# Router scores with the centroids as the stationary side and 512 tokens moving, turned back by TensorE

## The chip, the cores and the metric

One core of one Trainium2 chip runs the whole program in one launch. The metric is the device time of that core in microseconds, the median of several executions; lower is better.

## The reference, cut to what matters

The model takes 1024 tokens of 256 features and passes them through a feed-forward layer, attention, a second feed-forward layer, a mixture of experts, a Mamba layer and the same mixture of experts again. Ahead of each stands a layer norm. The change touches the router of the two mixtures:

```python
shared = _swiglu(x, wg_s, wu_s, wd_s) * RATIO
affinity = jax.nn.sigmoid(jnp.einsum('bsh,eh->bse', x, centroids))
biased = affinity + gate_bias
_, top_idx = jax.lax.top_k(biased, K)
top_aff = jnp.take_along_axis(affinity, top_idx, axis=-1)
weights = top_aff / (top_aff.sum(-1, keepdims=True) + EPS)
...
for e in range(E):
    routed = routed + mask[..., e:e + 1] * _swiglu(x, wg[e], wu[e], wd[e])
```

Here x is the normalised input, E is 16 experts, K is 2, and there are 256 features.

## The kernel before, in words

All engines walk one list of steps, `plan`, in the same order; each engine's program picks the steps it has a part in. So the order of the list is the order of every engine's queue. A step is a tuple such as `("route", u, ch)`: u is 0 for the first mixture and 1 for the last, ch is the half of the tokens (512 each, in TC = 4 tiles of 128).

A layer norm of one half is the steps of `norm_steps`: `stat` (VectorE, line 1561 and 1563: mean and variance of four tiles), `rstd` (GpSimd), `nrm` (VectorE, line 1574: four tiles, in two steps of two), `tr` (TensorE, line 489: eight 128x128 turns into two PSUM banks) and two `xn` (ScalarE, line 1326, copies a bank to `XN` as the high part; VectorE, line 1581, makes the low part from the difference). Products are made from high and low parts: `three` gives the pairs high-high, low-high, high-low, so a product over 256 features takes six matmuls (`group`, line 485).

`moe_steps(u)` orders the router. `mld` loads the centroids (VectorE splits them into `Cn`, 16 columns per 128 features) and the shared experts' weights. `route` is TensorE's: for each of four tiles six matmuls with the tokens' 128x128 tile of `XN` as the stationary side and the 16 centroid columns moving, 24 matmuls in all, so that the scores come out as 128 tokens by 16 experts in `bank(ch)`. `top` is ScalarE's sigmoid of 128x64 into `aff` (line 1375), and then VectorE's add of the bias (line 1687), the eight largest (line 1690) and their indices (line 1694). `rank` makes the one-hot rows (VectorE) and counts with 44 small matmuls (TensorE); `pos` turns the counts into row numbers (VectorE, lines 1716 to 1735). `scat` then writes the tokens to their experts' rows in memory, `GX`, by 16 indirect transfers that GpSimd issues one after another (lines 2005 and 2011). `fetch` (SyncE) reads them back, and `e1` to `e4` run the experts. Beside the scatter, the shared experts run: `sgu`, `smid`, `sdn`, and `sadd` (VectorE, line 1780) adds them to X. The first turn of `e1` waits for the first fetch and for `sadd`.

Before the change, the list is: `route` of half 0, the whole norm of half 1, `top` of half 0, then `route`, `top` and the rest of half 1.

Of the kernel before, what the change touches and what calls it, by code (L numbers as in the profile page):

```python
# [6 lines left out]
F = mybir.dt.float32  # L7
# [259 lines left out]
def moe_steps(u):  # L267
    s = 3 + 2 * u
    yield [("mld", u)]
    later = norm_steps(s, 1)  # L270
    yield [("route", u, 0)]
    for x in later:
        yield x
    yield [("top", u, 0)]
    yield [("route", u, 1), ("top", u, 1), ("rank", u), ("wsp", u)]
    yield [("sgu", u, 0, 0), ("pos", u), ("scat", u), ("wts", u)]
    yield [("sgu", u, 0, 1), ("smid", u, 0, 0), ("sgu", u, 1, 0), ("smid", u, 0, 1), ("sdn", u, 0, 0)]
    yield [("sgu", u, 1, 1), ("smid", u, 1, 0), ("sdn", u, 0, 1), ("smid", u, 1, 1), ("sdn", u, 1, 0), ("sdn", u, 1, 1)]
    yield [("sadd", u), ("fetch", u, 0), ("fetch", u, 1)]
    aside = iter([[x] for k in range(len(MW)) for x in (("mwl", k), ("mws", k))]) if u == 0 else iter(())  # L280
    n = len(PAIRS)
    for i in range(n + 3):
        if i < n:
            yield [("e1", u, i)]
            b = PAIRS[i][1]
            gi = (b - 1) // WB
            if i % 2 == 0:
                yield [("ids", u, gi)]
            if (b % WB == 0 or b == NB) and gi + 2 < len(GROUPS):
                yield [("fetch", u, gi + 2)]  # L290
        if 0 <= i - 1 < n:
            yield [("e2", u, i - 1)]
        if 0 <= i - 2 < n:
            yield [("e3", u, i - 2)]
        if 0 <= i - 3 < n:
            yield [("e4", u, i - 3), ("back", u, i - 3)]
        yield next(aside, [])
    after = norm_steps(4, 0)
    for h in range(NT // 2):
        yield [("yload", u, h)]  # L300
    for t in range(NT):
        yield [("comb", u, t)]
        if u == 0 and t >= TC:
            yield next(after)
    if u == 0:
        yield from after
        yield from norm_steps(4, 1)
# [111 lines left out]
def build(nc, d):  # L419
# [11 lines left out]
    with ctx:  # L431
# [3 lines left out]
        def sig(name, keys, step=1):  # L435
            return Sig(ctx.enter_context(nc.semaphore(name)), keys, step)
# [58 lines left out]
        ldc, ldb = sig("s_ld_cst", [()], 16), sig("s_ld_b16", [()], 16)  # L495
        pset = sig("s_pool_set", [("ones",), ("minus",), ("none",), ("mhalf",), ("zero",), ("b2h",)])
        gz = sig("s_gx_rows", [(0, "zero"), (0, "spare"), (1, "copy")], 16)
        asum = sig("s_abs", of("abs"))
        qsum = sig("s_abs_sum", of("sum"))
        wq = sig("s_wquant", of("quant"))  # L500
        con = sig("s_const", [()])
        var = sig("s_var", of("rstd"))
# [13 lines left out]
        tld = sig("s_ld_rope", [()], 16)  # L516
        awh, awq = sig("s_wqkvo_hi", [()]), sig("s_wqkvo", [()])
        vset = sig("s_v_pads", [()])
        kset = sig("s_k_pads", [()], 64)
# [45 lines left out]
        cen = sig("s_cen", of("mld"))  # L565
        rtd = sig("s_route", of("route"))
        sgm = sig("s_sigmoid", of("top"))
        hotd = sig("s_onehot", of("rank"))
# [125 lines left out]
        cenw = fa.take(32)  # L694
        bufs = [fa.take(CH) for _ in range(4)]
        small = Area(fa.take(1100), 1100)
        xin = [fa.take(WB * RW) for _ in range(2)]
# [63 lines left out]
        def sync_program():  # L761
            for x, *a in plan:
# [10 lines left out]
                elif x == "qld":  # L773
                    sp.wait_ge(*con.at())
                    sp.dma_start(wst, d["qkvo"]).then_inc(*qld.inc())
# [97 lines left out]
        def tensor_program():  # L873
# [31 lines left out]
            for x, *a in plan:  # L905
# [61 lines left out]
                elif x == "pj":  # L967
# [3 lines left out]
                    if (ch, w, u) == (0, "q", 0):  # L971
                        pe.wait_ge(*xad.at(0, 1))
                        pe.wait_ge(*awq.at())
                    for v in range(2):
# [18 lines left out]
                elif x in ("diag", "off"):  # L993
# [3 lines left out]
                    if x == "diag" and i == 0:  # L997
                        pe.wait_ge(*plc["q", g // 2].at(ch))
                        pe.wait_ge(*plc["k", g // 2].at(ch))
                        if ch:  # L1000
                            pe.wait_ge(*mzd[ch, g].at(ch, g))
                        if g == ch == 0:
                            pe.wait_ge(*kset.at())
                            pe.wait_ge(*qzero.at())
                            pe.wait_ge(*con.at())

# [63 lines left out]
                elif x == "route":  # L1070
                    u, ch = a
                    s = 3 + 2 * u
                    if ch == 0:
# [3 lines left out]
                        else:  # L1077
                            pe.wait_ge(*mlx.at(TC - 1))
                    pe.wait_ge(*xno.at(s, ch, 1))
                    for i in range(TC):  # L1080
                        A = [xn(k, ch, i * P, i * P + P) for k in range(2)]
                        t = group(bank(ch)[:, i * 16:i * 16 + 16], [q for k in range(2) for q in three(A[k], [w[:, k, :] for w in Cn])])
                    t.then_inc(*rtd.inc(u, ch))
                elif x == "rank":
# [6 lines left out]
                elif x == "sgu":  # L1091
# [3 lines left out]
                    if k0 == 0:  # L1095
                        pe.wait_ge(*wsl.at(u, 0))
                        pe.wait_ge(*sgm.at(u, 1))
                    elif k0 == 1:
                        pe.wait_ge(*posd.at(u))
                    else:  # L1100
                        pe.wait_ge(*smd.at(u, n - 1, ch))
# [212 lines left out]
        def scalar_program():  # L1314
            for x, *a in plan:
# [51 lines left out]
                elif x == "attT":  # L1367
# [3 lines left out]
                    act.activation(XN[:, 0, :, ch, :], bk, ACT.Copy).then_inc(*ath.inc(ch))  # L1371
                elif x == "top":
                    u, ch = a
                    act.wait_ge(*rtd.at(u, ch))
                    act.activation(aff[:, ch * TC:ch * TC + TC, :], bank(ch)[:, 0:16 * TC].rearrange("p (t e) -> p t e", e=16), ACT.Sigmoid).then_inc(*sgm.inc(u, ch))
                elif x == "wsp":
# [136 lines left out]
        def vector_program():  # L1513
# [6 lines left out]
            for x, *a in plan:  # L1520
# [17 lines left out]
                elif x == "const":  # L1538
# [3 lines left out]
                    dve.tensor_copy(TRI[:, :], b16[:, 256:512])  # L1542
                    dve.tensor_copy(BC16[:, :], b16[:, 0:256]).then_inc(*con.inc())
                elif x == "stat":
# [52 lines left out]
                elif x == "wq":  # L1597
                    dve.wait_ge(*awh.at())
                    dve.tensor_tensor(Wall[1], wst, Wall[0].bitcast(F), ALU.subtract).then_inc(*awq.inc())
                elif x == "rp1":  # L1600
# [18 lines left out]
                elif x == "vadd":  # L1619
# [4 lines left out]
                    if ch == n == 0:  # L1624
                        dve.wait_ge(*vset.at())
                    for v in range(2):
# [57 lines left out]
                elif x == "top":  # L1684
                    u, ch = a
                    dve.wait_ge(*sgm.at(u, ch))
                    dve.tensor_tensor(bi[:, ch * TC:ch * TC + TC, :], aff[:, ch * TC:ch * TC + TC, :], cst("gb").unsqueeze(1).broadcast_to([P, TC, 16]), ALU.add).then_inc(*d_own.inc())
                    dve.wait_ge(*d_own.at())
# [255 lines left out]
        def gpsimd_program():  # L1944
            for x, *a in plan:
# [26 lines left out]
                elif x == "wo":  # L1972
# [3 lines left out]
                    pool.wait_ge(*p_own.at())  # L1976
                    pool.memset(vv[:, :, 17:32], 0.0).then_inc(*vset.inc())
                elif x == "xbo":
# [157 lines left out]
```

## Time and profile before

| what | value |
|---|---|
| median of 3 runs | 938.44 us (932.56 to 939.86) |
| span of the profiled execution | 936.1 us |
| TensorE busy with matmuls | 713.1 us, 76% |
| VectorE, ScalarE, GpSimd busy | 592.4, 371.6 and 347.5 us |
| mean granted TensorE clock | 0.864 |

The span runs from the first to the last instruction of one execution. No time of that same execution from outside is among the numbers; its span lies 2.3 us under the median of the three runs and inside their spread. A granted clock of 1.0 is 2.4 GHz and one of 0.5 is 1.2 GHz.

### The profile page before, as it was taken

What the parts mean: (1) busy time and instruction counts of PE and PEld (TensorE: products, weight loads), DVE (VectorE), ACT (ScalarE), POOL (GpSimd) and SP (SyncE); (2) the same over time, 40 slices, a digit from 0 to 9 for tenths busy, and PEclk for the clock granted to TensorE, in tenths of its full rate; (3) what the DMA queues carried; (4) which work ended last, traced back from release to release, by engine and by line L of the source; (5) the groups of instructions that cost most, each with busy time, mean ns of one, the idle gap of its engine ahead of it and who ended that gap; (6) DMA issues with size and microseconds to landing.
All of it is one profiled execution on the core that took longest, in us unless ns stands there. A gap on an engine that the chain in (4) does not pass through costs nothing. (4 is left out here: it accounts for less than half of the span.)

```text
span 936.1 us, 11120 instructions
## 1 busy us (share of the span) xinstructions
PE 713.1 (76%) x3706; PEld 492.4 (53%) x3706; DVE 592.4 (63%) x1012; ACT 371.6 (40%) x754; POOL 347.5 (37%) x422
## 2 busy tenths in 40 slices
PE   3887887889885987599248578888778879675990
PEld 2766453444333766488146345545445545564880
DVE  6868445767522776344367686788988798662333
ACT  4411334255563322033124844586544444130330
POOL 3223222201112202536310055566656667124462
PEclk9989677779888895899769679999999999867995
DMA  4945622020001910364400000000051000103435
GB/s 179 284 62 94 82 36 37 2 35 2 1 1 55 392 35 13 122 184 165 146 1 0 1 0 1 1 1 1 1 216 54 1 0 1 35 24 129 129 123 174
DMA packets 37640, 65.98 MB, mean 70 GB/s; under 512 B 11618, under 2 KB 27618, under 8 KB 35954
## 3 DMA queue, kind: packets, MB, share of 16 engines
q1 hardware_dynamic: 33074, 52.89, 20.1%
q0 software_dynamic: 4512, 12.39, 3.7%
q8 instruction: 31, 0.51, 0.2%
q14 instruction: 23, 0.19, 0.1%
HBM read 39.65 MB, written 21.69 MB: 66 GB/s over the span
## 5 line engine op out<-in xcount | busy, mean ns | idle before, releaser
L1260 PE MATMUL PS<-FB,C 128*128 128x512 f32 x256 | 134.5, 621 | 4.2 <-DVE FB L1919 3.8
L1360 ACT ACTIVATE FA<-PS 128x512 f32<-128x512 f32 (+3 forms) x192 | 80.7, 496 | 71.5 <-PE PS L1030 71.1
L2045 POOL TENSOR_TENSOR FB<-FB,RBF 128x512 f32<-128x512 f32 x51 | 65.8, 1289 | 81.8 <-DVE FB L1910 81.8
L489 PE MATMUL PS<-C,FB 128*128 128x128 f32 x250 | 45.3, 305 | 57.2 <-DVE FB L1574 30.8
L1996 POOL TENSOR_SCALAR_AFFINE_SELECT FA<-FA 128x128 f32<-128x128 f32 x128 | 36.4, 295 | 129.1 <-ACT FA L1360 126.9
L2026 POOL DMA_INDIRECT GY<-FB x62 | 60.7, 979 | 53.7 <-issue 27.5
L1642 DVE TENSOR_REDUCE FA<-PS 128x2 f32<-128x1024 f32 (+2 forms) x64 | 68.0, 1086 | 19.6 <-PE PS L1009 19.4
L489 PEld LDWEIGHTS PS<-C,FB 128*128 128x128 f32 x250 | 35.6, 158 | 68.5 <-DVE FB L1574 30.9
L1030 PE MATMUL PS<-RA 64*128 64x512 f32 (+3 forms) x192 | 60.2, 496 | 5.4 <-ACT FA L1360 4.9
L1153 PE MATMUL PS<-WE,FB 128*128 x248 | 61.0, 390 | 0.0
L2036 POOL TENSOR_TENSOR FB<-WE,FB 128x512 f32<-128x512 f32 x32 | 42.4, 1325 | 49.3 <-ACT FB L1468 49.3
L1260 PEld LDWEIGHTS PS<-FB,C 128*128 128x128 f32 x256 | 45.9, 198 | 21.1 <-issue 11.8
L1030 PEld LDWEIGHTS PS<-RA 64*128 64x128 f32 x192 | 29.1, 222 | 52.7 <-ACT FA L1360 30.3
L485 PE MATMUL PS<-XN,RB 128*128 128x512 f32 x192 | 52.5, 433 | 2.3 <-issue 2.3
L1790 DVE TENSOR_TENSOR FB<-FB,PS 128x256 f32<-128x256 f32 (+1 forms) x32 | 13.2, 413 | 64.2 <-ACT FB L1398 52.0
L1009 PE MATMUL PS<-RA 64*128 64x128 f32 (+3 forms) x288 | 49.7, 385 | 4.7 <-DVE FA L1642 2.7
L1044 PE MATMUL PS<-FA 128*32 128x512 f32 (+3 forms) x384 | 47.8, 576 | 4.0 <-POOL FA L1996 3.9
L1153 PEld LDWEIGHTS PS<-WE,FB 128*128 128x128 f32 x248 | 46.1, 196 | 6.1 <-issue 0.8
L485 PEld LDWEIGHTS PS<-XN,RB 128*128 128x128 f32 x192 | 40.1, 212 | 12.6 <-issue 3.2
L1249 PEld LDWEIGHTS PS<-RBF,WE 128*128 128x128 f32 x256 | 35.5, 203 | 20.4 <-DVE FB L1910 7.5
L1326 ACT ACTIVATE XN<-PS 128x512 fp32r<-128x512 f32 x24 | 13.5, 594 | 76.5 <-PE PS L489 76.5
L485 PE MATMUL PS<-XN,W1Q 128*128 128x512 f32 x128 | 39.3, 445 | 5.1 <-DVE XN L1581 3.6
(265 smaller groups left out, 1628.1 us busy)
## 6 DMA issues: line engine op xcount, KB each, us to landing
WE<-in_wr SPq DMA_DIRECT2D x8, 1536.0 KB, 11.3
FB<-GX SPq DMA_DIRECT2D x14, 520.0 KB
RA<-RA SPq DMA_DIRECT2D x48, 128.0 KB, 4.8
FB<-GY SPq DMA_DIRECT2D x8, 512.0 KB, 5.7
GX<-GX SPq DMA_DIRECT2D x1, 4030.0 KB, 27.6
GX<-FA SPq DMA_DIRECT2D x1, 3968.0 KB, 16.7
FA<-in_w SPq DMA_DIRECT2D x2, 1024.0 KB, 7.0
FA<-in_qkvo SPq DMA_DIRECT2D x1, 1536.0 KB, 20.6
```

The source lines that it names most:

```text
L485: last = pe.matmul(out, a, b, start=start and i == 0, stop=stop and i == len(pairs) - 1, skip_group_check=skip)
L489: return pe.matmul(out, in_, ident, start=True, stop=True, is_transpose=True)
L1009: return pe.matmul(out, QT[r, 2 * g + hh // 2, ii * P:ii * P + P], KT[r, 2 * g + hh // 2, c0:c1], start=start, stop=stop, skip_group_check ...
L1030: pe.matmul(bk[:, c0:CH], KT[r, 2 * g + hh // 2, kt * P:kt * P + P], QT[r, 2 * g + hh // 2, c0:CH], start=True, stop=True).then_inc(*scs.i ...
L1044: t = pe.matmul(bank(7)[32 * hh:32 * hh + 32, c0:CH], V[:, kt, (4 * g + hh) * 32:(4 * g + hh) * 32 + 32], PT[(first_of + hh) % 12][:, c0:C ...
L1153: m = pe.matmul(bk[:, o:o + D], xt[:, o + k * P:o + k * P + P], WE[:, bass.ds(v + k * 256, 256)], start=k == 0, stop=k == 1)
L1260: pe.matmul(bank(m), ident, shc[k % 4], start=n == 0, stop=n == DN - 1).then_inc(*yad.inc(ch, n, m))
L1360: act.activation(PT[n % 12][:, c0:], bank(ring_bank[(x, *a)])[:, c0:], ACT.Exp, scale=0.25).then_inc(*exd.inc(*a))
L1642: r = dve.reduce_max(N3[c0 // CH][:, i, h:h + 2 * hpb].rearrange("p (h b) -> p b h", b=2), bk[:, :, 0:hpb * n].rearrange("p b (h n) -> p b ...
L2026: pool.indirect_dma_start(GY, bass.IndirectOffsetOnAxis(ap=ids[:, b:b + 1], axis=0), yout[pi % 4][:, (b - b0) * D:(b - b0) * D + D], None) ...
L2036: pool.tensor_tensor(sbb[k % 2], uu[ch][:, m, :], bs[(stb.no[ch, n] - 1) % 2], ALU.mult).then_inc(*bmd.inc(ch, n, m))
L2045: pool.tensor_tensor(shc[k % 4], sh[k % 5], Cs[(stc.no[ch, n] - 1) % 2], ALU.mult).then_inc(*cma.inc(ch, n, m))
```

## The change

The router's product is turned round. `route` now takes the 16 centroid columns as the stationary side and moves 512 tokens past them: six matmuls for each half, with a result of 16 experts by 512 tokens. ScalarE takes the sigmoid of that 16x512 block (into `affT`, a part of two buffers that are free then). In `top`, TensorE turns the block back, four turns of 16x128 to 128x16, and VectorE adds the bias to the turned affinities in PSUM, copies them to `aff` for later use, and makes the choices as before. In the list, the statistics and both `nrm` steps of half 1 now stand right after `route` of half 0, and `top` of half 0 stands ahead of `tr` and both `xn`. Some semaphores are merged into others; each wait still names the same event.

```diff
-    later = norm_steps(s, 1)
     yield [("route", u, 0)]
-    for x in later:
-        yield x
-    yield [("top", u, 0)]
+    stat0, stat1, rstd, nrm0, nrm1, tr, xn0, xn1 = norm_steps(s, 1)
+    yield stat0 + stat1 + rstd + nrm0 + nrm1
+    yield [("top", u, 0)] + tr + xn0 + xn1
     yield [("route", u, 1), ("top", u, 1), ("rank", u), ("wsp", u)]
...
-        rtd = sig("s_route", of("route"))
-        sgm = sig("s_sigmoid", of("top"))
+        rtd = sig("s_route", [x for x in plan if x[0] in ("route", "top")])
+        sgm = sig("s_sigmoid", of("route"))
+        afd = sig("s_affinity", of("top"))
...
+        affT = [b[0:16, :] for b in bufs[2:4]]
...
                     pe.wait_ge(*xno.at(s, ch, 1))
+                    group(bank(ch)[0:16, :], [q for k in range(2) for q in three([w[:, k, :] for w in Cn], xn(k, ch))]).then_inc(*rtd.inc(x, u, ch))
+                elif x == "top":
+                    u, ch = a
+                    pe.wait_ge(*sgm.at(u, ch))
                     for i in range(TC):
-                        A = [xn(k, ch, i * P, i * P + P) for k in range(2)]
-                        t = group(bank(ch)[:, i * 16:i * 16 + 16], [q for k in range(2) for q in three(A[k], [w[:, k, :] for w in Cn])])
-                    t.then_inc(*rtd.inc(u, ch))
+                        t = pe.matmul(bank(ch)[:, i * 16:i * 16 + 16], affT[ch][:, i * P:i * P + P], ident[0:16, 0:16], start=True, stop=True, is_transpose=True)
+                    t.then_inc(*rtd.inc(x, u, ch))
...
                     if k0 == 0:
                         pe.wait_ge(*wsl.at(u, 0))
-                        pe.wait_ge(*sgm.at(u, 1))
+                        pe.wait_ge(*afd.at(u, 1))
...
-                elif x == "top":
+                elif x == "route":
                     u, ch = a
-                    act.wait_ge(*rtd.at(u, ch))
-                    act.activation(aff[:, ch * TC:ch * TC + TC, :], bank(ch)[:, 0:16 * TC].rearrange("p (t e) -> p t e", e=16), ACT.Sigmoid).then_inc(*sgm.inc(u, ch))
+                    act.wait_ge(*rtd.at(x, u, ch))
+                    act.activation(affT[ch], bank(ch)[0:16, :], ACT.Sigmoid).then_inc(*sgm.inc(u, ch))
...
-                    dve.wait_ge(*sgm.at(u, ch))
-                    dve.tensor_tensor(bi[:, ch * TC:ch * TC + TC, :], aff[:, ch * TC:ch * TC + TC, :], cst("gb").unsqueeze(1).broadcast_to([P, TC, 16]), ALU.add).then_inc(*d_own.inc())
+                    turned = bank(ch)[:, 0:16 * TC].rearrange("p (t e) -> p t e", e=16)
+                    dve.wait_ge(*rtd.at(x, u, ch))
+                    dve.tensor_tensor(bi[:, ch * TC:ch * TC + TC, :], turned, cst("gb").unsqueeze(1).broadcast_to([P, TC, 16]), ALU.add).then_inc(*d_own.inc())
+                    dve.tensor_copy(aff[:, ch * TC:ch * TC + TC, :], turned).then_inc(*afd.inc(u, ch))
```

## Rows read from the trace of the kernel before

**Rows 1.** Chain that ended last, last mixture: start us, us, what.

```profile
809.66 3.18 DMA FB<-in_cen
...
813.32 4.54 PE PS L485 x24
...
821.48 5.30 PE PS L485 x24
826.80 0.23 ACT FB L1375
...
834.28 0.72 POOL FB L2002
...
857.92 3.52 DMA FB<-GX
```

**Rows 2.** Timeline, first mixture: start us, us, engine, line, op, tiles, count, idle before.

```profile
348.82 4.27 PE L485 MATMUL PS<-RB,XN 128*128 128x16 f32 x24 [3.61 <-DVE RB L1518]
...
352.39 1.38 DVE L1574 TENSOR_SCALAR FB<-X,FB 128x256 f32<-128x256 f32 x4 [1.48 <-POOL FB L1964]
...
353.18 1.97 PE L489 MATMUL PS<-C,FB 128*128 128x128 f32 x8
...
355.60 1.29 DVE L1581 TENSOR_TENSOR XN<-PS,XN 128x512 fp32r<-128x512 f32 x2 [1.83 <-ACT XN L1326]
...
356.94 5.29 PE L485 MATMUL PS<-RB,XN 128*128 128x16 f32 x24 [1.80 <-DVE XN L1581]
...
357.62 0.23 DVE L1687 TENSOR_TENSOR FB<-FB,C 128x64 f32<-128x64 f32 x1 [0.73 <-ACT FB L1375]
...
358.84 0.17 DVE L1694 FIND_INDEX8 FB<-FB 128x8 uint32<-128x16 f32 x1
...
362.53 0.23 DVE L1687 TENSOR_TENSOR FB<-FB,C 128x64 f32<-128x64 f32 x1 [3.52 <-ACT FB L1375]
```

**Rows 3.** Stretches, TensorE alone: us, busy (count), granted clock, DMA share, GB/s.

```profile
349.80:350.00 0.20, 0.20 (x4) 0.91 0.95 323
...
350.00:370.20 20.20, 15.73 (x101) 0.50 0.03 12
...
370.20:386.00 15.80, 14.72 (x84) 0.99 0.23 84
```

**Rows 4.** Timeline, shared experts' first and third `sgu`, on TensorE and ScalarE.

```profile
363.97 1.28 ACT L1385 ACT_TABLE_LOAD   x1
...
366.01 7.85 PE L485 MATMUL PS<-XN,RB 128*128 128x512 f32 x24
...
368.96 0.60 ACT L1385 ACTIVATE FB<-PS 128x512 f32<-128x512 f32 x1 [3.70 <-PE PS L485]
...
374.94 3.06 PE L485 MATMUL PS<-XN,RB 128*128 128x512 f32 x12 [1.08 <-issue]
...
376.64 0.60 ACT L1385 ACTIVATE FB<-PS 128x512 f32<-128x512 f32 x1 [3.55 <-PE PS L485]
```

**Rows 5.** Groups by line and shape: count, busy us, mean ns, idle before.

```profile
L1352 ACT ACTIVATE RA<-PS 8x512 fp32r<-8x512 f32 x8 | 4.7, 587 | 22.1 <-PE PS L489 22.1
...
L485 PE MATMUL PS<-W1Q,RB 128*64 128x512 f32 x16 | 5.9, 442 | 0.0
```

**Rows 6.** Timeline, four turns and the copy behind them, first and last mixture.

```profile
401.72 0.57 PEld L489 LDWEIGHTS PS<-C,FB 128*128 128x128 f32 x4
...
402.57 0.60 ACT L1392 ACTIVATE FB<-PS 128x512 f32<-128x512 f32 x1
...
861.48 1.57 PEld L489 LDWEIGHTS PS<-C,FB 128*128 128x128 f32 x8 [10.63 <-DMA FB<-GX]
...
862.64 0.60 ACT L1392 ACTIVATE FB<-PS 128x512 f32<-128x512 f32 x1 [16.64 <-PE PS L489]
```

**Rows 7.** Timeline, end of the first mixture's scatter and start of its experts.

```profile
393.91 2.74 DVE L1780 SCALAR_TENSOR_TENSOR X<-PS,X 128x256 f32<-128x256 f32 x8 [9.72 <-remote]
...
397.23 1.97 PE L489 MATMUL PS<-C,FB 128*128 128x128 f32 x8 [10.71 <-DMA FB<-GX]
```

More of the change, by code:

```diff
@@ L495, in build @@
         ldc, ldb = sig("s_ld_cst", [()], 16), sig("s_ld_b16", [()], 16)
-        pset = sig("s_pool_set", [("ones",), ("minus",), ("none",), ("mhalf",), ("zero",), ("b2h",)])
+        pset = sig("s_pool_set", [("ones",), ("minus",), ("none",), ("mhalf",), ("zero",), ("b2h",), ("vpad",)])
         gz = sig("s_gx_rows", [(0, "zero"), (0, "spare"), (1, "copy")], 16)
@@ L499, in build @@
         qsum = sig("s_abs_sum", of("sum"))
-        wq = sig("s_wquant", of("quant"))
-        con = sig("s_const", [()])
+        wq = sig("s_wquant", of("quant") + [("const",), ("qkvo",)])
         var = sig("s_var", of("rstd"))
@@ L516, in build @@
         tld = sig("s_ld_rope", [()], 16)
-        awh, awq = sig("s_wqkvo_hi", [()]), sig("s_wqkvo", [()])
-        vset = sig("s_v_pads", [()])
+        awh = sig("s_wqkvo_hi", [()])
         kset = sig("s_k_pads", [()], 64)
@@ L773, in sync_program @@
                 elif x == "qld":
-                    sp.wait_ge(*con.at())
+                    sp.wait_ge(*wq.at("const"))
                     sp.dma_start(wst, d["qkvo"]).then_inc(*qld.inc())
@@ L972, in tensor_program @@
                         pe.wait_ge(*xad.at(0, 1))
-                        pe.wait_ge(*awq.at())
+                        pe.wait_ge(*wq.at("qkvo"))
                     for v in range(2):
@@ L1004, in tensor_program @@
                             pe.wait_ge(*qzero.at())
-                            pe.wait_ge(*con.at())
+                            pe.wait_ge(*wq.at("const"))
                     def score(out, ii, hh, c0, c1, start, stop):
@@ L1542, in vector_program @@
                     dve.tensor_copy(TRI[:, :], b16[:, 256:512])
-                    dve.tensor_copy(BC16[:, :], b16[:, 0:256]).then_inc(*con.inc())
+                    dve.tensor_copy(BC16[:, :], b16[:, 0:256]).then_inc(*wq.inc("const"))
                 elif x == "stat":
@@ L1598, in vector_program @@
                     dve.wait_ge(*awh.at())
-                    dve.tensor_tensor(Wall[1], wst, Wall[0].bitcast(F), ALU.subtract).then_inc(*awq.inc())
+                    dve.tensor_tensor(Wall[1], wst, Wall[0].bitcast(F), ALU.subtract).then_inc(*wq.inc("qkvo"))
                 elif x == "rp1":
@@ L1624, in vector_program @@
                     if ch == n == 0:
-                        dve.wait_ge(*vset.at())
+                        dve.wait_ge(*pset.at("vpad"))
                     for v in range(2):
@@ L1976, in gpsimd_program @@
                     pool.wait_ge(*p_own.at())
-                    pool.memset(vv[:, :, 17:32], 0.0).then_inc(*vset.inc())
+                    pool.memset(vv[:, :, 17:32], 0.0).then_inc(*pset.inc("vpad"))
                 elif x == "xbo":
```

## The prediction

> **What bounds the kernel now.** I read the chain that ended last first, because one router stands in each mixture and only its share of the chain can be won. In the last mixture the chain goes from the load of the centroids through the first scores, the norm of half 1, the 24 matmuls of the second scores (5.30 us), ScalarE's sigmoid and the choices to GpSimd's first piece of the scatter, and from the scatter to the fetch [rows 1]. The second `route` is thus wholly on the path, and what is saved between the end of `xn` and the bias add moves the scatter, the fetch and all behind them. The first mixture has the same shape, and there I read the timeline piece by piece [rows 2]. VectorE ends the low parts at 355.60 + 1.29 = 356.89, TensorE's 24 matmuls run from 356.94 to 362.23, and the bias add starts at 362.53. From 356.89 to 362.53 are 5.64 us. That is the stretch the change rebuilds, twice in the program; the last mixture's has the same 5.29 us or so of TensorE in it [rows 1].
>
> Next I looked at the clock, since a matmul's price depends on it. It falls from 1.0 at about 350.0, one microsecond into the first `route`, after TensorE had been idle 3.61 us [rows 2, 3]. It then stays at 0.5 (1.2 GHz) until 370.2, 4.2 us after the first `sgu` began, and is 0.99 after that [rows 3, 4]. So the second `route` and all that stands beside it run at 1.2 GHz.
>
> **The second half's scores, on the path.** What goes is 5.64 us. What comes, in order:
>
> - Six matmuls of 512 columns. `sgu` has just such a group of six for its gate: at 1.2 GHz it starts at 366.01 and ScalarE takes its result at 368.96, 2.95 us; at 2.4 GHz it starts at 374.94 and is taken at 376.64, 1.70 us [rows 4]. Their stationary side has 128 columns, the new one 16. The nearest row with fewer columns is the one with 64, at 442 ns mean duration and 5.9 us for 16, which is 0.37 us each and lies between the two speeds of the full-width group (0.49 and 0.28 us per matmul with start and drain in it) [rows 4, 5]. I take no gain and no loss from the width. With 0.05 us from VectorE to TensorE (356.89 to 356.94 [rows 2]) this is 3.00 us.
> - The sigmoid of 16x512. ScalarE's cost follows the columns and not the partitions: 8x512 from PSUM takes 587 ns, 128x512 takes 0.60 [rows 4, 5]. I take 0.60, and 0.05 again for the way to TensorE.
> - Four turns of 16x128. No row has this form. The nearest is the four 128x128 turns of `e1`: from the first weight load to the copy behind them 1.16 us at 1.2 GHz (861.48 to 862.64) and 0.85 us at 2.4 GHz (401.72 to 402.57) [rows 6]. The new ones load as many columns (128) but move 16 in place of 128. From below they can't be quicker than the 24 loads of the old `route`, which had the same 128 columns to load and 16 to move: 5.29/24 = 0.22 us each, 0.88 us for four [rows 2]. The range is 0.9 to 1.2; I take 1.15, since start and drain are not in the 0.88.
> - The add of 128x64 costs what it did (0.23 us), now from PSUM. Behind it comes the copy to `aff`, of the same size, ahead of the maxima in VectorE's queue: at most another 0.23 us, less some overlap; I take 0.20 [rows 2].
>
> The sum is 3.00 + 0.60 + 0.05 + 1.15 + 0.20 = 5.00 us, against 5.64: 0.64 us saved in each mixture at 1.2 GHz, 1.3 us in both. With the lower bound for the turns and a copy half hidden it is 1.0 each; with a new group slower by a quarter of its matmul time (0.7 us) it is a loss of 0.1 each.
>
> The Trainium skill has a rule that speaks against the change (TensorE: Matmul & The Clock Gate, section on LDWEIGHTS): a weight load costs its columns divided by 1.2 in ns, whatever the clock, here 107 ns. By that, 24 loads would be 2.6 us, the six long matmuls would win nothing and the change would lose its sigmoid, turns and copy, over a microsecond. The trace does not agree: the old group took 0.22 us for each load and matmul at 1.2 GHz.
>
> **The first half's scores, beside other work.** TensorE's 24 matmuls there end at 353.09, and the turns of the norm start at 353.18, when VectorE has two of its four tiles [rows 2]; in the last mixture `route` ends at 817.86 and the turns follow at once, so there it may hold them up by 0.1 us [rows 1]. The new group starts at the same 348.8, gets its first microsecond or so at 2.4 GHz and ends after about 2.2 us, at 351.0 (2.95 at the latest, 351.8). The sigmoid is then done by 351.7 (352.4), the turns by 352.8 (353.6). ScalarE is free in this stretch. Its table for the sigmoid costs 1.28 us, but a table load does not wait for the data: the one for Silu stands at 363.97, five microseconds ahead of the result it serves at 368.96 [rows 4]. So it goes into ScalarE's idle time before 348.8. TensorE is then free at 352.8 for the norm's turns, which can't start before 353.1. I cost all this at nothing; if that cover were gone, the late sum (353.6) would hold the norm's turns up by 0.5 us per mixture.
>
> **Where VectorE's choices for half 0 go.** They took from 357.62 to 359.01, 1.39 us, beside the second `route`, where VectorE had nothing else [rows 2]. Now they and the copy, 1.6 us, stand between `nrm` (ends 352.39 + 1.38 = 353.77) and the first low part (355.60), where VectorE idled 1.83 us for ScalarE's high part [rows 2]. From 353.77 they end at 355.37, which leaves 0.2 us. Behind VectorE's new wait for the turned scores are queued both low parts, and TensorE's second `route` waits for those. I cost it at nothing, and each tenth beyond 0.2 us goes straight onto the path.
>
> **What hangs behind.** GpSimd starts the scatter when the positions are there, and is its own bound from then on: 16 issues in a row. SyncE's fetch follows the last, and the experts start at 397.23 when it lands [rows 7]. All that is relative to the choices and moves with them. The shared experts' `sgu` also starts earlier by as much. One stretch is not clear: `sadd` starts at 393.91 after 9.72 us of waiting for something the profile does not name, and ends at 396.65, 0.58 us ahead of the fetch [rows 7]. If that wait hangs on the scatter, it moves too; if it hangs on something that stays, no more than 0.58 us can be won in this mixture, nearly all of my 0.64. Merged semaphores cost nothing: no wait has a new event.
>
> The profiled execution's span is 936.1 us; less 1.3 and a tenth for the last mixture's turns it is 934.7. Its span lies 2.3 under the median of 938.44, so the median becomes 937.0.
>
> **The rivals.** First, the clock comes back during the second `route`. The old group ran 5.29 us without a rise [rows 2, 3]. For it: the clock rose 4.2 us after `sgu` began, with matmuls of just the new length [rows 3, 4]. Against it: the new group lasts only some 2.6 us and then TensorE pauses for ScalarE. At 2.4 GHz the stretch is 0.05 + 1.70 + 0.60 + 0.05 + 0.85 + 0.20 = 3.45 us, 2.2 saved in each mixture, 4.4 in all: 934.0. The Trainium skill's rule (TensorE: Matmul & The Clock Gate, Part 1) that the clock is low by default and that activity releases it would allow this; the rise during `sgu` agrees, the level during the old `route` shows that not every busy stretch does it.
>
> Second, slower: VectorE's queue. If the turned scores of half 0 come later than 354.0, so that choices and copy (1.6 us) end after 355.60, the low parts wait. It decides from a chain of 5.2 us from 348.8 on; my late sum of 353.6 is 0.4 short of it. Should narrow-sided matmuls cost half as much again (6 x 0.64 in place of 0.43 us, 1.3 more for a group), the scores of half 0 would come at 354.9, the low parts 0.9 us late (354.9 + 1.6 against 355.60), and the second half's group would be 1.3 us longer, against 0.64 saved: 1.6 us lost in each mixture, 3.1 in all, 941.5. The row with 64 columns speaks against it [rows 5].
>
> Third, the change does what it says but `sadd` or the experts' start holds the place: nothing moves, 938.4.
>
> **How the numbers follow.** Forecast 0.62; clock back, 934.0, 0.15; VectorE's queue, 941.5, 0.08; nothing moves, 0.15. Around each lies the spread of the runs, 7.3 us for three of them, and the time at which the clock rises in later stages can shift by some microseconds with any edit. All four cases are within 1% (9.4 us), which is about what a measurement of this kernel can tell from no change. Beyond it lie only disturbed medians: 0.04 faster, 0.03 slower. For 8 in 10 the range takes in 934.0 less the spread's lower half and 937.0 and 938.4 plus a little of the upper: 930.5 to 940.5; most of the slower rival is left out.
>
> **What would show it.** In the profile after: two groups of six 128x512 matmuls with 16 stationary columns per mixture, the second at a granted clock of 0.5, with ScalarE's sigmoid some 2.95 us behind its start; sigmoid 0.6 us; the bias add 4.8 us after the end of the low parts; the choices of half 0 ahead of the low parts with idle time before the latter under 0.3 us; the experts' first turns about 0.6 us nearer to the centroids' load. A clock of 1.0 there, or low parts that wait for VectorE's own choices, would make me wrong, and so would a `sadd` that ends after the fetch.

## The result and the profile after

The changed kernel takes 929.11 us in the median (924.94 to 932.21, 8 runs) against 937.64 for the kernel before beside it (931.94 to 939.86, 8 runs). The ratio is 0.9918, with a 95% interval of 0.989 to 0.9947: 5.0 to 10.3 us faster, where 1.4 us was forecast. The profiled execution took 925.12 us and its span is 923.8 us. It happens to be one of the quickest, so the difference of the two spans, 12.3 us, is not the gain.

The first mixture's router in the changed kernel's timeline (start us, us, engine, line, op, tiles, count, idle before; PS stands for PSUM banks, PEld is TensorE loading its stationary side):

```profile
343.02 2.69 PE L484 MATMUL PS<-XN,RB 128*16 128x512 f32 x6 [3.73 <-DVE RB L1520]
...
345.75 0.59 ACT L1377 ACTIVATE FB<-PS 16x512 f32<-16x512 f32 x1 [7.12 <-PE PS L484]
...
346.38 0.60 PE L1084 MATMUL PS<-C,FB 16*128 16x16 f32 x4 [0.68 <-ACT FB L1377]
346.58 1.38 DVE L1576 TENSOR_SCALAR FB<-X,FB 128x256 f32<-128x256 f32 x4 [1.47 <-POOL FB L1968]
...
347.88 0.22 DVE L1690 TENSOR_TENSOR FB<-PS,C 128x64 f32<-128x64 f32 x1
348.01 0.22 DVE L1691 COPY FB<-PS 128x64 f32<-128x64 f32 x1
...
349.80 1.29 DVE L1583 TENSOR_TENSOR XN<-PS,XN 128x512 fp32r<-128x512 f32 x2 [0.54 <-ACT XN L1328]
...
351.14 2.74 PE L484 MATMUL PS<-XN,RB 128*16 128x512 f32 x6 [1.80 <-DVE XN L1583]
...
353.92 0.59 ACT L1377 ACTIVATE FB<-PS 16x512 f32<-16x512 f32 x1 [3.67 <-PE PS L484]
...
354.56 0.61 PE L1084 MATMUL PS<-C,FB 16*128 16x16 f32 x4 [0.68 <-ACT FB L1377]
...
355.20 0.23 DVE L1690 TENSOR_TENSOR FB<-PS,C 128x64 f32<-128x64 f32 x1 [4.12 <-PE PS L1084]
355.34 0.22 DVE L1691 COPY FB<-PS 128x64 f32<-128x64 f32 x1
355.47 0.40 DVE L1694 MAX8 FB<-FB 128x8 f32<-128x16 f32 x4
```

Read it against [rows 2]. From the end of the low parts (349.80 + 1.29 = 351.09) to the bias add at 355.20 VectorE is idle for 4.12 us by its row, where the stretch was 5.64 and I had summed 4.80 to that point. The sum's terms, one by one: the group is taken 2.78 us after its start (351.14 to 353.92; I had 2.95), the sigmoid is 0.59, and from the first turn to VectorE's add are 0.64 us, where I had 1.15. The copy, for which I had 0.20, costs the path 0.01: the maxima start 0.27 us after the add (355.20 to 355.47), and in the kernel before, without a copy, they start 0.26 us after it (362.53 to 362.79), since they wait for the add's result in both:

```profile
362.79 0.41 DVE L1690 MAX8 FB<-FB 128x8 f32<-128x16 f32 x4
```

The choices of half 0 start at 347.88, in VectorE's own order behind the four tiles, and VectorE is idle 0.54 us before the low parts: the queue holds nobody up.

The chain that ended last, at the last mixture's router (start us, us, what), and two lines of the timeline there:

```profile
799.65 1.55 DMA FB<-in_cen
...
809.25 2.75 PE PS L484 x6
812.02 0.60 ACT FB L1377
812.66 0.62 PE PS L1084 x4
813.31 0.23 DVE FB L1690
```

```profile
801.69 1.55 PE L484 MATMUL PS<-XN,RB 128*16 128x512 f32 x6 [2.53 <-DVE RB L1520]
...
806.05 1.30 PE L488 MATMUL PS<-C,FB 128*128 128x128 f32 x8 [1.71 <-DVE FB L1576]
```

Against [rows 1], three things are shorter, not one. The scores go as in the first mixture. But the load of the centroids takes 1.55 us in place of 3.18, though nobody touched it. And the norm's turns take 1.30 us where the first mixture needs 1.97 [rows 2]: they run at 2.4 GHz. The stretches with TensorE alone (us, busy, count, granted clock, DMA share, GB/s), first the kernel before, then the changed one, both from just after the split of the centroids:

```profile
813.60:817.60 4.00, 4.00 (x23) 0.57 0.01 4
```

```profile
802.00:806.00 4.00, 1.66 (x10) 1.00 0.35 136
```

What became of the load is told by the list of transfers in that stretch (queue, kind: packets, MB, share; then issues with KB and us to landing), again before and after:

```profile
q1 hardware_dynamic: 430, 0.80, 47.3%
q8 instruction: 1, 0.02, 1.3%
...
FB<-in_cen SPq DMA_DIRECT2D x1, 16.0 KB, 3.2
```

```profile
q1 hardware_dynamic: 432, 0.80, 46.9%
...
FB<-in_cen SPq DMA_DIRECT2D x1, 16.0 KB, 1.6
```

In the kernel before, one packet of instructions crosses the load; in the changed one there is none. That became the first theory to test: the edit took 28 matmuls with their weight loads out of TensorE's program ahead of this point (the first mixture's two halves have 10 each in place of 24), and so moved the packet away.

### The profile page after: what moved, and what is told of

Read it like the earlier page. It is cut to its first block and busy times, and to the rows that moved or that the text cites. A ratio compares the mean times of both kernels' runs of the same rounds, so it can differ in the third digit from the quotient of the medians.

```text
span 923.8 us, 11012 instructions
## 1 busy us (share of the span) xinstructions
PE 697.1 (75%) x3650; PEld 472.3 (51%) x3650; DVE 594.7 (64%) x1016; ACT 372.4 (40%) x754; POOL 351.2 (38%) x422
## 5 line engine op out<-in xcount | busy, mean ns | idle before, releaser
L484 PE MATMUL PS<-XN,RB 128*128 128x512 f32 (+1 forms) x216 | 61.1, 441 | 12.0 <-DVE RB L1520 8.3
L1029 PE MATMUL PS<-RA 64*128 64x512 f32 (+3 forms) x192 | 57.6, 466 | 5.2 <-ACT FA L1362 5.1
L484 PEld LDWEIGHTS PS<-XN,RB 128*128 128x128 f32 (+1 forms) x216 | 41.8, 198 | 26.8 <-DVE RB L1520 9.6
L1251 PE MATMUL PS<-RBF,WE 128*128 128x128 f32 x256 | 37.3, 293 | 6.0 <-DVE RBF L1914 3.6
```

Source lines behind the costliest of these rows:

```text
L484: last = pe.matmul(out, a, b, start=start and i == 0, stop=stop and i == len(pairs) - 1, skip_group_check=skip)
L1029: pe.matmul(bk[:, c0:CH], KT[r, 2 * g + hh // 2, kt * P:kt * P + P], QT[r, 2 * g + hh // 2, c0:CH], start=True, stop=True).then_inc(*scs.i ...
L1251: t = pe.matmul(bank(4 + k % 2)[:, i * P:i * P + P], DUT[ch][i][:, m * P:m * P + P], dg[:, i * P:i * P + P], start=True, stop=True)
```

## The experiments

Twelve runs in three groups of four, four of them repeats; each group shares its runs of the kernel before (medians 935.95, 936.72 and 933.62 us). My theory: 1.5 us in each mixture by the scores, the last mixture's load and clock, and nothing else. The rivals: the merged semaphores, the order of the steps, or something that acts ahead of the first router, where the two profiles already differ by 5.8 us (first statistics of the first mixture at 348.71 and 342.91).

**Merged semaphores alone.**

```diff
-        wq = sig("s_wquant", of("quant"))
-        con = sig("s_const", [()])
+        wq = sig("s_wquant", of("quant") + [("const",), ("qkvo",)])
...
```

> Only the merged semaphores, with the old router. Theory 1 (the gain is made between the end of the low parts and the scatter, 1.5 and 2.1 us in the two profiles, and what lies beyond is the clock of stages that the change does not touch): no change, ratio 1.000 within 0.003, and the stages before the first router (chain at the first bias of the centroids, 348.36 before and 342.56 after) differ from both kernels only as one execution differs from another. Theory 2 (the merged semaphores shorten the waits of the first feed-forward layer and attention): the kernel is 4 to 6 us faster, ratio 0.994 to 0.996, and reaches the first router near 342.5.

936.79 us, ratio 1.0018 (0.9985 to 1.0051): no gain. Its profile nevertheless reaches the first statistics at 343.53.

**The order alone.**

```diff
     yield [("route", u, 0)]
-    for x in later:
-        yield x
-    yield [("top", u, 0)]
+    yield stat0 + stat1 + rstd + nrm0 + nrm1
+    yield [("top", u, 0)] + tr + xn0 + xn1
```

> Only the order: old router, statistics and both norm steps of half 1 ahead of the choices of half 0, which stand ahead of the turns. The old scores of half 0 end 4.3 to 4.5 us after their start and the sigmoid is 0.2 us, so the choices start when VectorE has finished its four tiles, as in the changed kernel, and end before the low parts. Theory 1: no gain from the order, 0 to -0.2 us in each mixture, ratio 1.000 within 0.003. Rival (the order is what gains, since VectorE is free beside the second scores): 1 to 3 us faster.

937.01 us, ratio 1.0018 (0.9987 to 1.005): no gain. Low parts to bias add stay at 5.64 us in both mixtures.

**The turned product alone**: the diff of the change with the old list of steps, and with all but one of the merged semaphores separate again.

> Only the turned product, in the old order, with one merged semaphore, as one more is needed than there are. Theory 1: 1.5 us in the first mixture and about 2 in the last, 3.5 us in all, ratio 0.9963 (0.993 to 0.999). Then second scores to bias add 4.1 us against 5.64. But the choices of half 0 stand behind the low parts of half 1 and beside the second scores, which now end early: they take 1.5 us from 351.1 on, the new scores need 4.1, so they still fit. Rival (the gain needs the order too): half of it or less.

927.76 us, ratio 0.9925 (0.989 to 0.9959). The product alone carries the whole gain, and its profile has 4.12 and 4.11 us for the scores and 1.95 us from X to the statistics in the last mixture, as the changed kernel's. The rival that it needs the order fell.

**The changed kernel again, beside them.**

> The changed kernel again, on the chip and beside the runs that the three parts share. Theory 1: ratio 0.991 to 0.996; if the parts are additive it is the product of the three others. If it is again near 0.992 while the parts give 0.996 together, something acts only in the whole.

931.32 us, ratio 0.9935 (0.99 to 0.9969). The product of the three parts' ratios is 0.9961, inside this interval, so nothing that acts only in the whole is needed; the intervals are too wide to exclude 1 or 2 us of it.

**The instruction packet put back.** TensorE gets 28 small matmuls in a time in which it waits for the first fetch.

```diff
                     m.then_inc(*sdn.inc(u, n, ch))
+                    if (u, n, ch) == (0, 1, 1):
+                        for _ in range(28):
+                            pe.matmul(bank(2)[:, 0:16], TRI[:, 0:P], mb[:, 0, :], start=True, stop=True)
```

> The changed kernel with 28 small matmuls more (each with its weight load) in TensorE's idle time between the first mixture's shared experts and its first fetch, 0.9 us of work that nobody waits for. They give TensorE's program the length that it had at the last mixture's router before the change. Theory (the last mixture's load of the centroids took 3.2 us in each kernel with the old router and 1.6 in each with the turned one because a 16 KB packet of TensorE's instructions, which the old program's length puts there, shares the transfer engines with it): load 3.0 to 3.4 us again, clock down before the norm's turns again (end of the split of the centroids to end of the low parts 8.5 us against 7.96), 2.2 us slower than the changed kernel, ratio 0.994 to 0.997. Rival (the load is shorter because of what the turned router itself does): load 1.6 us, ratio as the changed kernel's.

The load's rows, from the list of transfers and the timeline of the changed kernel with the 28 matmuls, and two stretches with TensorE alone:

```profile
q8 instruction: 1, 0.02, 1.0%
...
FB<-in_cen SPq DMA_DIRECT2D x1, 16.0 KB, 3.0
```

```profile
809.28 0.18 DVE L1521 CAST RB<-FB 128x32 fp32r<-128x32 f32 x1 [3.04 <-DMA FB<-in_cen]
...
821.74 0.23 DVE L1693 TENSOR_TENSOR FB<-PS,C 128x64 f32<-128x64 f32 x1 [3.93 <-PE PS L1084]
```

```profile
820.00:821.00 1.00, 0.61 (x2) 0.60 0.00 0
821.00:822.00 1.00, 0.42 (x4) 1.00 0.00 0
```

The packet is back and the load takes 3.0 us. The norm of half 1 takes 8.18 us again from its first statistics to the end of the low parts, in place of 7.62. As a time, 930.65 us and ratio 0.9933 (0.9896 to 0.9969) can't be told from the changed kernel's 0.9935, and so the forecast of 2.2 us slower is not shown by the times. The profile also has something on the other side: the scores take 3.93 us, not 4.12, since the clock rose to 1.0 near 820.8, 0.2 us behind the second group (817.87 to 820.61) and before the turns (821.28), which then took 0.42 us in place of 0.61.

**The same 28 matmuls in the kernel before.**

> The kernel before with the same 28 matmuls in the same idle time. Theory of the instruction packet: the packet comes some ten microseconds earlier and misses the load, which takes 1.6 us; the last mixture gains 1.6 us and 0.6 by the clock, so that a kernel with more work is 2.2 us faster, ratio 0.997 to 0.998. The second scores keep their 5.64 us. Rival: load 3.2 us, ratio 1.000.

```profile
810.01 0.33 SPq L829 DMA_DIRECT2D FB<-in_cen  x1
811.59 0.18 DVE L1519 CAST RB<-FB 128x32 fp32r<-128x32 f32 x1 [1.61 <-DMA FB<-in_cen]
...
812.06 3.26 PE L485 MATMUL PS<-RB,XN 128*128 128x16 f32 x24 [2.53 <-DVE RB L1521]
```

With the old router and more instructions, the load takes 1.6 us and the transfers in that stretch show no packet of instructions. The packet is there in all five profiles with a load of 3.0 to 3.4 us (the four with the old router in their plain form, and the changed kernel with the 28 matmuls) and in none of the six with one of 1.6 or 1.7. So the length of TensorE's program decides and not the router. The clock's 0.6 us did not come with it: the norm takes 8.18 us. For that the short load is not enough in the kernel before. The time, 935.04 us and ratio 0.9996 (0.9959 to 1.0033), shows neither.

**The centroids loaded once, early**, with the old router.

```diff
+        CEN = sb("CEN", [P, 64], R)
...
                     sp.dma_start(b16, d["b16"]).then_inc(*ldb.inc())
+                    sp.dma_start(cenw, d["cen"]).then_inc(*ldm.inc())
...
                     dve.tensor_copy(HOT[:, :], cst("hot"))
+                    dve.wait_ge(*ldm.at())
+                    split(CEN[:, 0:32], CEN[:, 32:64], cenw).then_inc(*cen.inc())
...
-                    sp.dma_start(cenw, d["cen"]).then_inc(*ldm.inc(u))
```

> The kernel before with the centroids loaded and split once, at the start, into a place of their own (384 bytes a partition), for both mixtures; the routers no longer wait for a load. Statistics then start as soon as X is there: 1.7 us saved in the first mixture and 3.2 in the last, and the clock keeps 2.4 GHz longer, as TensorE doesn't idle four microseconds: 0 to 0.6 us for the norm's turns in each, and up to 2.6 for the second scores if it is kept until then. 5 to 8 us faster, ratio 0.991 to 0.995. Theory of the sum: second scores to bias add still 5.64 us when the clock is down by then.

928.2 us, ratio 0.9917 (0.988 to 0.9954). That is as much as the whole change won. By the profile, the time from the last addition to X to the first statistics shrinks by 2.0 us in the first mixture (2.04 to 0.03) and by 3.6 in the last, 5.6 us in all. The scores keep 5.64 us, as expected.

**Early load and turned router together**, twice.

> The changed kernel with the same early load of the centroids. Against the kernel before with the early load this is the turned router alone, without the load that an instruction packet can hit: 1.5 us in each mixture, 3 in all. Against the changed kernel: 1.7 and 1.6 us, and 0.6 in the first mixture if the clock holds until the norm's turns. 928 to 925 us, ratio 0.986 to 0.991 to the kernel before.

> The version with both the turned router and the early load again, as it had 6 runs only: ratio 0.985 to 0.992, and not slower than the changed kernel. By the sum it saves 5.3 us (the change) less what both save (the last load), plus 1.7 and 1.6 us: about 8 us, ratio 0.991.

926.41 us, ratio 0.9897 (0.9845 to 0.995), and again 925.62 us, ratio 0.9879 (0.9818 to 0.994): 4.7 to 14.5 us and 5.6 to 17.0 us faster than the kernel before, the best of all versions, though its interval overlaps the changed kernel's. In its first mixture:

```profile
340.31 1.55 PE L486 MATMUL PS<-XN,CEN 128*16 128x512 f32 x6 [1.56 <-issue]
...
344.73 1.30 PE L490 MATMUL PS<-C,FB 128*128 128x128 f32 x8 [1.78 <-DVE FB L1581]
...
347.94 2.74 PE L486 MATMUL PS<-XN,CEN 128*16 128x512 f32 x6 [1.90 <-DVE XN L1588]
```

TensorE waits only 1.56 us there, where it waited 3.73, and the clock lasts through the norm's turns, but is down when the second group comes (2.74 us). In the last mixture of both runs it went the other way: no load is waited for there either, yet the norm takes 8.18 us and in the first run's profile the clock fell to 0.5 at about 803.5 us, as the turns began (803.54). So a short wait for the load is not enough to keep the clock with the new router either; what else decides when it falls was not found.

**Full turns.**

```diff
-                    act.activation(affT[ch], bank(ch)[0:16, :], ACT.Sigmoid).then_inc(*sgm.inc(u, ch))
+                    act.activation(affT[ch], bank(ch)[:, :], ACT.Sigmoid).then_inc(*sgm.inc(u, ch))
...
-                        t = pe.matmul(bank(ch)[:, i * 16:i * 16 + 16], affT[ch][:, i * P:i * P + P], ident[0:16, 0:16], start=True, stop=True, is_transpose=True)
+                        t = turn_over(bank(ch)[:, i * P:i * P + P], affT[ch][:, i * P:i * P + P])
```

> The changed kernel with full turns: the sigmoid over all 128 partitions of the bank and four turns of 128x128 with the 128 identity columns moving, in place of 16x128 with 16. This prices the term of the sum that I took too high (1.15 us, from full turns). If the size of the block is what makes them cheap: sigmoid 0.60 as before, turns and way to VectorE 1.1 to 1.2 us at 1.2 GHz against 0.65, low parts to bias add 4.6 us against 4.12, 1 us slower in both mixtures together. If full turns cost the same here: 4.12 again.

928.37 us, ratio 0.9931 (0.989 to 0.9971). The timeline, first mixture and then last:

```profile
355.38 0.60 ACT L1377 ACTIVATE FB<-PS 128x512 f32<-128x512 f32 x1 [3.67 <-PE PS L484]
356.03 0.71 PEld L488 LDWEIGHTS PS<-C,FB 128*128 128x128 f32 x4 [1.59 <-ACT FB L1377]
...
357.18 0.22 DVE L1690 TENSOR_TENSOR FB<-PS,C 128x64 f32<-128x64 f32 x1 [4.64 <-PE PS L488]
...
807.45 1.57 PE L484 MATMUL PS<-XN,RB 128*16 128x512 f32 x6 [1.90 <-DVE XN L1583]
...
809.05 0.60 ACT L1377 ACTIVATE FB<-PS 128x512 f32<-128x512 f32 x1 [2.49 <-PE PS L484]
...
810.86 0.23 DVE L1690 TENSOR_TENSOR FB<-PS,C 128x64 f32<-128x64 f32 x1 [3.46 <-PE PS L488]
```

In the first mixture four full turns take 356.03 to 357.18, 1.15 us, my term to the hundredth, and the scores 4.64 us. So full turns do cost 1.15, and the small block costs little over half as much. The edit changed two things in the turns, the partitions loaded and the columns moved, and the single instructions tell which of them counts (least, median and longest ns; small turns of the changed kernel, full turns of this run's first mixture, and the old second `route` of the kernel before):

```profile
L1084 PEld LDWEIGHTS PS<-C,FB x16: 135/219/220, 346.4 to 812.9; 16*128 16x128 f32 x16
...
L1084 PE MATMUL PS<-C,FB x16: 207/263/285, 346.4 to 813.0; 16*128 16x16 f32 x16
```

```profile
L488 PEld LDWEIGHTS PS<-C,FB x4: 183/226/229, 356.0 to 356.5; 128*128 128x128 f32 x4
...
L488 PE MATMUL PS<-C,FB x4: 417/417/473, 356.0 to 356.7; 128*128 128x128 f32 x4
```

```profile
L485 PEld LDWEIGHTS PS<-RB,XN x24: 288/333/333, 356.9 to 361.8; 128*128 128x128 f32 x24
```

The load of 16 partitions lasts 219 ns and that of 128 partitions 226: that is not it. The matmul lasts 263 ns with 16 columns moving and 417 with 128. The old route's loads are slower than either, 333 ns each.

In the last mixture the clock held until the second group, which then took 1.60 us (807.45 to 809.05), in one of the six profiles of kernels with the turned router and the loads in their old place. It fell to 0.5 at 808.9, and the full turns ran at 1.2 GHz (1.16 us). The scores took 3.46.

**Both kernels once more**, one execution each.

> The kernel before once more, for a second profile of its stages outside the routers. Theory (what differs ahead of the first router is one execution against another): the first statistics of the first mixture may start near 343.5 or near 348.7, as in the profiles so far, which fall into two groups whatever the kernel. The scores keep 5.64 us and the last load of the centroids 3.0 to 3.4 us. Rival (the changed kernel is quicker ahead of its first edit): near 348.7 again.

> The changed kernel once more, for a third profile. Either group ahead of the first router; low parts to bias add 4.12 us in both mixtures, the last load of the centroids 1.6 us, start of the last statistics to end of the low parts 7.62 us.

```profile
342.72 5.29 PE L485 MATMUL PS<-RB,XN 128*128 128x16 f32 x24 [3.76 <-DVE RB L1518]
...
350.28 1.29 DVE L1581 TENSOR_TENSOR XN<-PS,XN 128x512 fp32r<-128x512 f32 x2 [2.62 <-ACT XN L1326]
```

The unchanged kernel now has its first statistics at 342.60, the changed one at 344.01. The changed kernel's repeat in the first group has 348.11. So the rival is out: each kernel has been seen in both groups, and what the two first profiles differ by ahead of the router is not the change. These two repeats ran on another chip than the first eight (13 and not 1), but chip 1 has both kinds too: 343.53 with the merged semaphores, 348.11 with the changed kernel. What causes the 5 to 6 us was not found. The rows show something that the first profile hid: when the clock is already down as the first group starts, the 24 old matmuls take the full 5.29 us and end at 348.01, after VectorE has its tiles, and the low parts start 0.8 us later in the norm than in [rows 2] (idle 2.62 against 1.83 us).

All profiles side by side, in us, worked out from starts and ends in the timelines. "Load" is the last mixture's time from the last addition to X to the first statistics; "norm" is from the first statistics to the end of the low parts, "scores" from there to the bias add, for the first and the last mixture.

```
kernel                        load    norm          scores
before                        3.58    8.18  8.21    5.64  5.64
before, again                 3.60    8.97  8.40    5.64  5.64
merged semaphores             3.78    8.65  8.55    5.64  5.64
order                         3.41    8.18  8.22    5.64  5.64
before + 28 matmuls           1.96    8.18  8.18    5.63  5.64
before + early load             -     8.20  8.18    5.64  5.64
after                         1.95    8.18  7.62    4.12  4.11
after, in the first group     1.95    8.19  7.62    4.12  4.12
after, again                  2.11    8.18  7.61    4.12  4.11
turned product                1.95    8.18  7.62    4.12  4.11
after + 28 matmuls            3.39    8.18  8.18    3.93  3.93
after + early load              -     7.64  8.18    4.12  3.93
after + early load, again       -     7.63  8.18    4.12  3.93
full turns                    2.06    8.18  7.62    4.64  3.46
```

## Why the prediction was wrong

The direction was right and so was one place of the gain; the size was not: 1.4 us forecast, 5.0 to 10.3 measured, and the time of 929.11 lies under the range's end of 930.5. Two steps failed: the turns' price in the sum, with its lower bound, and the load of the centroids with the norm behind it, which the sum put at nothing.

- *The scores on the path.* The first step that failed is the term for the four turns: "from below they can't be quicker than the 24 loads of the old `route`, which had the same 128 columns to load and 16 to move". They were: 0.64 us against my floor of 0.88 and my value of 1.15. The bound took the old route's loads for the turns' loads, but those last 333 ns each and the turns' 219; whether the data format or the turning makes that difference was not tried. The value of 1.15 was read from full turns, and the run with full turns gave just that; their 128 moving columns cost the rest. The copy cost 0.01 for 0.20, as the maxima waited for the add anyway. The group took 2.78 for 2.95: the row that I read begins with the last 0.15 us of the 44 counting matmuls (they end at 366.16 and `sgu` starts at 366.01), and without them it gives 2.80. Together the stretch is 1.52 us shorter in each mixture up to the bias add, 1.51 to the maxima, and not 0.64: 0.51 of the difference by the turns, 0.19 by the copy and 0.17 by the group.
- *The width.* No gain or loss from 16 columns was nearly right: 2.74 us of matmul time for six at 1.2 GHz, 1.55 at 2.4.
- *What stands ahead.* This is the second step that failed. The sum had no term for the load. I had its 3.18 us in [rows 1], and VectorE's wait of 1.69 us for the same load in the first mixture stood in the same trace, and I did not ask why one program's same load should differ. The difference was 1.6 us on the path. Putting the 28 matmuls back took it away (load 3.0 us) and adding 28 to the kernel before won it (1.6 us), both in one profile each; the times of those two runs are too spread to show it.
- *The first half's scores.* I cost their removal at 0.1 us for the last mixture. It is 0 to 0.8, by when the clock falls (norm 8.18 to 8.97 with the old router), and in every profile that has both the new group and the short load in the last mixture the clock lasts through the norm's turns (7.62), 0.6 us. The two with the early load, where it did not (8.18), show that this is a finding of these runs and not a rule.
- *VectorE's queue.* Right that it fits. The low parts wait for ScalarE and not for the choices.
- *The clock rival.* Mostly absent: the second group ran at 1.2 GHz in the first mixture of all eight profiles with the turned product, and in the last mixture of seven. In the eighth, the 3.46 us measured look like the 3.45 worked out for the rival, but that is luck: the rival's sum has 0.20 for a copy behind the bias add and small turns at 2.4 GHz, and the measured stretch ends at the bias add and has full turns at 1.2 GHz. The group alone can be compared: 1.60 us for 1.70. The Trainium skill says (TensorE: Matmul & The Clock Gate, Part 1) that activity releases the throttle. The rise in the kernel with 28 more matmuls, 0.2 us behind a group that kept TensorE busy for 2.74 us, fits that; the same 2.74 us in the changed kernel's first mixture brought no rise, with the clock still at 0.5 from 354 to 358 us.
- *What hangs behind.* The scatter and the fetch move with the choices, as forecast: from the issue of the centroids' load to the experts' first turns are 48.86 us in the first mixture (340.77 to 389.63) where they were 50.54 (346.69 to 397.23). The scatter's 21.35 us from first to last issue are 20.80 in the first profile after and 21.32 in the second. The worry about `sadd` came from something that only the first profile of the kernel before shows. There it starts 7.4 us after TensorE's last product for it (386.52 to 393.91). In the second profile of the same kernel, and in all twelve others, it waits 2.4 us for TensorE and ends well ahead of the fetch, in the changed kernel at 379.25 + 2.74 = 381.99 against a fetch issued at 385.86. It does not hang on the scatter and holds nothing up; what it waited for in the first profile stays open.
- *The rule on weight loads.* The Trainium skill's formula (TensorE: Matmul & The Clock Gate, LDWEIGHTS), which it gives without a clock, makes 107 ns of a load of 128 columns, and by that the change would have lost. It gained: the old loads last 333 ns each at 1.2 GHz, and the second group took 5.29 us in the first mixture of every profile with the old router. Here the measurement differs from the page, and it decides.

The ledger from the two first profiles: scores 1.52 and 1.53, load 1.63, norm 0.59, together 5.3 us, ratio 0.9944. That is inside the intervals of the result (just), of its repeat and of the turned product alone. It also says something on the miss: with 5.3 us less than the 937.64 beside it the changed kernel would stand at 932.3, inside the range, and its repeat, 931.32, did. So the two failed steps make the gain four times the forecast, and the 3.2 us from 932.3 to 929.11, which put the median outside the range, are not explained by them. Medians of one kernel differ by as much: 929.11 and 931.32 for the changed one, 933.62 to 937.64 for the one before. The quickest execution of the turned product, 924.37, lies 5.9 us under the quickest of the 35 runs of the kernel before beside it, 930.22. The medians lie 8.5, 8.2 and 4.6 us apart. Whether something of 1 to 3 us is still beyond the ledger was not settled; the runs can't tell it from their spread. In the other direction, the last mixture's experts, from the bias add to the end of VectorE's last addition, took 106.4 to 107.2 us in the six profiles with the old scores and 106.7 to 109.0 in the eight with the new, 1.2 us more in the mean, which takes back part of the ledger's 5.3; why was not tried.

## What to carry to other kernels

In a product with few output columns it can pay to make these columns the stationary side: here, with 16 columns stationary and 512 tokens moving, six matmuls replaced 24 and won 1.5 us of 5.6 even with the turns back. Price a small form from a row of its own kind of instruction, and call a bound from another kind a guess: the floor of 0.88 us for the turns was none. Before pricing an edit, compare the same transfer at its places in one trace; a difference that the code does not explain may move with an edit that is far from it. A load of constants that stands alone on the path is worth taking off it before its neighbours are tuned: here it gave as much as the whole change (ratio 0.9917 and 0.9918).

## What the runs showed that was not expected

- A 16 KB packet of instructions that crosses a 16 KB load of data made it 3.0 to 3.4 us in place of 1.6. 28 matmuls added or taken some 400 us earlier moved the packet onto the load or off it.
- Four turns of 16x128 took 0.61 us at 1.2 GHz and 0.42 at 2.4; four of 128x128 took 1.15 us to VectorE's start, where the small ones took 0.64. The loads of both last about the same (219 and 226 ns); the matmuls do not (263 and 417).
- ScalarE's sigmoid of 16x512 took 0.59 us and that of 128x512 0.60: eight times the partitions cost 0.01 us.
- With an unchanged program, the time up to the first router differs by 6.1 us between two executions (342.60 and 348.71), most of the 7.1 us by which their spans differ (929.0 and 936.1).
